# A graph attention kernel: which of the gathered tiles TensorE picks itself, one in 40 instead of one in 16

## What is computed

```python
for Wl, bl, Wr, br, att, bo, g, be in layers:            # three times
    xl = (h @ Wl + bl).reshape(n, H, C)                  # H * C = 128
    xr = (h @ Wr + br).reshape(n, H, C)
    x_i = xl[dst]                                        # neighbours in the sorted list
    x_j = xr[src]                                        # any row: a gather
    logit = einsum('ehc,hc->eh', leaky_relu(x_i + x_j, 0.2), att)
    alpha = softmax of logit over the edges of one dst
    out = segment_sum(alpha[..., None] * x_j, dst)
```

## Time and profile before

| | us |
|---|---|
| median of 3 runs (6605.31 to 6611.03) | 6605.85 |
| the profiled execution's own time | 6615.38 |
| its span, first to last instruction | 6613.6 |
| granted TensorE clock, mean over the span | 0.841 |
| PE busy | 4770.9 (72%) |
| DVE busy | 3963.6 (60%) |
| POOL busy | 3805.8 (58%) |
| ACT busy | 1607.7 (24%) |

### The profile page before, as it was taken

How to read it: one execution, slowest core, us unless ns; L and a number is a source line. 1 busy time by engine, 2 the same in 40 slices (tenths; PEclk the granted TensorE clock), 3 DMA queues, 4 the chain that set the end, 5 groups by cost and what they waited for, 6 DMA issues and landing times. The chain is left out here.

```text
span 6613.6 us, 138303 instructions
## 1 busy us (share of the span) xinstructions
PE 4770.9 (72%) x35731; PEld 4233.1 (64%) x35732; DVE 3963.6 (60%) x9254; ACT 1607.7 (24%) x3395; POOL 3805.8 (58%) x3122
## 2 busy tenths in 40 slices
PE   7878774888888748888887478888874566666665
PEld 5755334777787647778776478777773455555555
DVE  8987226666666576666665766666666533333334
ACT  4764100111111111111111111111111134444443
POOL 0000003777777737777777277777771078888884
PEclk9999986898999878999998789898886777777777
DMA  6853442333333323333333233333331222222221
GB/s 163 220 161 110 121 119 56 87 93 91 97 97 94 96 68 87 92 96 96 93 94 97 69 82 97 92 94 91 92 99 42 52 69 65 65 66 66 65 65 46
DMA packets 640422, 603.10 MB, mean 91 GB/s; under 512 B 245196, under 2 KB 579098, under 8 KB 639526
## 3 DMA queue, kind: packets, MB, share of 16 engines
q0 software_dynamic: 248480, 231.25, 15.1%
q10 hardware_dynamic: 234095, 211.99, 11.0%
q1 hardware_dynamic: 157719, 158.28, 9.0%
HBM read 498.50 MB, written 99.35 MB: 90 GB/s over the span
## 5 line engine op out<-in xcount | busy, mean ns | idle before, releaser
L563 POOL DMA_INDIRECT rows<-row_table,now x2250 | 2783.6, 1237 | 1780.7 <-issue 1505.8
L563 POOL DMA_INDIRECT rows<-node_table,now x800 | 989.0, 1236 | 563.5 <-issue 563.5
L850 PE MATMUL turn<-xr,ft 125*125 125x132 f32 x7500 | 969.7, 286 | 70.5 <-DVE ft L920 69.2
L850 PEld LDWEIGHTS turn<-xr,ft 125*125 125x125 f32 x7500 | 936.3, 197 | 76.2 <-DVE ft L920 71.1
L951 DVE SCALAR_TENSOR_TENSOR z<-zp,own 125x512 f32<-125x512 f32 x672 | 464.1, 691 | 780.8 <-PE zp L831 775.7
L842 PEld LDWEIGHTS sums<-both,hot 125*125 125x125 f32 x5376 | 765.5, 198 | 179.3 <-issue 117.4
L842 PE MATMUL sums<-both,hot 125*125 125x137 f32 x5376 | 795.5, 293 | 99.1 <-ACT both L737 57.7
L831 PE MATMUL zp<-rows,ident 125*125 x2700 | 809.9, 426 | 37.7 <-SPq L588 37.7
L828 PE MATMUL zp<-parts,hot_t 125*125 x8100 | 649.9, 232 | 240.2 <-issue 190.1
L828 PEld LDWEIGHTS zp<-parts,hot_t 125*125 125x125 bf16 x8100 | 607.9, 144 | 275.0 <-issue 273.2
L736 ACT CAST hot<-hot 125x500 f32<-125x500 bf16 x672 | 408.7, 608 | 1510.8 <-PE sums L842 898.8
(11 more groups left out here) (454 smaller groups left out, 5572.7 us busy)
## 6 DMA issues: line engine op xcount, KB each, us to landing
hot<-hots ACTq DMA_DIRECT2D x896, 122.1 KB
hot_t<-hots_t ACTq DMA_DIRECT2D x678, 122.1 KB
counts<-pairs SPq DMA_DIRECT2D x55, 685.1 KB
rows<-row_table,now POOLq DMA_INDIRECT x2250, 3.6
spread_slots<-slot_table POOLq DMA_DIRECT2D x56, 488.3 KB, 5.4
hots_t<-hot_t SPq DMA_DIRECT2D x112, 218.8 KB
hots<-hot_dst SPq DMA_DIRECT2D x112, 218.8 KB
pairs<-cells SPq DMA_DIRECT2D x25, 685.1 KB
```

Source lines behind the costliest of these rows:

```text
L563: pool.indirect_dma_start(rows[:, q, j, :], None, table, bass.IndirectOffsetOnAxis(ap=now[:, n, lane + j:lane + j + 1], axis=0)).then_inc( ...
L850: ins = pe.matmul(mixture, hot_n[:, w, :], xr[:, w, :], start=w == 0, stop=w == WIN - 1)
```

## The change

A tile is picked in every tenth quad instead of every fourth, so that TensorE makes 20 tiles per attention layer instead of 50, and POOL gathers 780 instead of 750. In blocks 0 to 8 the picks stand in the first two of the four groups of steps (`PER = 2`); blocks 9 to 13 have none. Two tiles are still made ahead of block 0 (`FIRST = 2`). The loops over a block's groups are split on all engines into groups with and without a pick. The list of picked sources, made once in the first stage, is cut from the other half of each row of 1000 edges, so that one small instruction there works on 250 numbers per partition instead of 125 (L1984), and the list's place in memory moved.

```diff
-PICK = 4
+PICK = 10
+PER = 2
+FIRST = 2
 PICKS = QUADS // PICK
-LAST = (PICKS - 2) // GROUP
+LAST = (PICKS - FIRST) // PER
...
-            def load_srcs(t, n=GROUP):
+            def load_srcs(t, n=PER):
...
+            def block_of(b, per):
+                if per:
+                    with act.Fori(0, per) as i:
+                        group(b, i)
+                        store_picked(PER * b + i + FIRST)
+                if per < GROUP:
+                    with act.Fori(per, GROUP) as i:
+                        group(b, i)
                 weigh(b)
...
-            def block_of(b, picking, picked_by):
-                four_steps(b, 0, softmax(b - 1, picked_by=picked_by), picking)
-                with pe.Fori(1, GROUP) as i:
-                    four_steps(b, i, None, picking)
+            def block_of(b, per, picked_by):
+                four_steps(b, 0, softmax(b - 1, picked_by=picked_by), per > 0)
+                if per > 1:
+                    with pe.Fori(1, per) as i:
+                        four_steps(b, i)
+                if per < GROUP:
+                    with pe.Fori(max(per, 1), GROUP) as i:
+                        four_steps(b, i, None, False)
                 sum_rows(BSTEPS * b - 1, AHEAD - 1)
 
             with pe.Fori(1, LAST) as b:
-                block_of(b, True, GROUP * b + 2)
+                block_of(b, PER, PER * b + FIRST)
             with pe.Fori(LAST, BLOCKS) as b:
-                block_of(b, False, PICKS)
+                block_of(b, 0, PICKS)
...
+            def block_of(b, per):
+                both(b, 0, per > 0)
+                if per > 1:
+                    with dve.Fori(1, per) as i:
+                        both(b, i, True)
+                if per < GROUP:
+                    with dve.Fori(max(per, 1), GROUP) as i:
+                        both(b, i, False)
...
-    g.picked_src = nc.dram_tensor("picked_src", (PICKS + GROUP, P), F16, kind="Internal").ap()
     g.picked_rows = nc.dram_tensor("picked_rows", (PICKS, P, ROW), F32, kind="Internal").ap()
     g.features = nc.dram_tensor("features", (D, N), F32, kind="Internal").ap()
+    g.picked_src = nc.dram_tensor("picked_src", (PICKS + PER, P), F16, kind="Internal").ap()
...
-                sp.dma_start(g.picked_src[0:PICKS, :], src16[1:RROWS:2, :]).then_inc(kept, 16)
+                sp.dma_start(g.picked_src[0:PICKS, :], src16[4:RROWS:5, 1, :]).then_inc(kept, 16)
...
-                link(dve.tensor_scalar(src16[:, :], src_row[:, rlen - P:rlen], float(-(N // 2)), None, ALU.add))
+                link(dve.tensor_scalar(src16[:, :, :], src_row[:, :].rearrange("r (h e) -> r h e", h=2)[:, :, rlen // 2 - P:rlen // 2], float(-(N // 2)), None, ALU.add))
```

More of the change, by code:

```diff
@@ L48 @@
 EPS = 1e-5
[L49 removed]
+PICK = 10
+PER = 2
+FIRST = 2
 PICKS = QUADS // PICK
 CUTS = ((0, 9), (9, 17), (17, WIN))
[L52 to L53 removed]
+LAST = (PICKS - FIRST) // PER
+assert RING % PICK == 0 and FIRST <= GROUP and PER <= GROUP and E // RROWS == 2 * HALF * P and FIRST + PER * LAST == PICKS and LAST < BLOCKS - 1
 GROUPS = (WIN + 3) // 4
@@ L761, in weigh @@
                 act.wait_ge(soft, SOFT * b + SOFT)
-            load_srcs(0, 2)
+            load_srcs(0, FIRST)
             for q in range(2):
                 load_spread(q, q)
-            lay(0, 2)
+            lay(0, FIRST)
             act.wait_ge(laid, 1)
-            load_srcs(2)
-            for t in range(2):
+            load_srcs(FIRST)
+            for t in range(FIRST):
                 store_picked(t)
@@ L772, in _, with spreads @@
             act.wait_ge(laid, 2)
-            load_srcs(GROUP + 2)
-            with act.Fori(0, GROUP) as i:
+            load_srcs(PER + FIRST)
+            def spreads(i):
                 for q in range(AHEAD):
                     load_spread(AHEAD * i + q + 2, (q + 2) % AHEAD)
-                store_picked(i + 2)
+            with act.Fori(0, PER) as i:
+                spreads(i)
+                store_picked(i + FIRST)
+            if PER < GROUP:
+                with act.Fori(PER, GROUP) as i:
+                    spreads(i)
             for q in range(2):
@@ L780, in _, with group @@
             weigh(0)
[L782 to L790, removed]
+            def group(b, i):
+                for q in range(AHEAD):
+                    k, c = BSTEPS * b + AHEAD * i + q, BSTEPS * b + AHEAD * i + q - BSTEPS
+                    widen(c, GROUP * b + i - GROUP, i, q)
+                    load_spread(k + 2, (q + 2) % AHEAD)
+                    load_hot(c + 2, (q + 2) % AHEAD)
+            def block_of(b, per):
[6 more added lines that the diff above has]
+                        group(b, i)
                 weigh(b)
@@ L878, in four_steps @@
                     k = BSTEPS * b + AHEAD * i + q
-                    if q or not isinstance(i, int):
+                    if q or not (isinstance(i, int) and i == 0):
                         sum_rows(k - BSTEPS - 1, (q - 1) % AHEAD)
@@ L883, in four_steps @@
                     if picking and q:
-                        pick(GROUP * b + i + 2, q - 1)
+                        pick(PER * b + i + FIRST, q - 1)
                     spread_rows(k + 1, GROUP * b + i + (q + 1) // AHEAD, (q + 1) % AHEAD, places[q])
-            for t in range(2):
+            for t in range(FIRST):
                 for r in range(len(CUTS)):
@@ L1029, in _, with alone @@
             dve.wait_ge(laid, 2)
-            with dve.Fori(0, GROUP) as i:
+            def alone(i, picking):
                 for q in range(AHEAD):
-                    choose(0, i, q)
+                    if picking:
+                        choose(0, i, q)
                     for _ in logits(AHEAD * i + q, i, q):
                         pass
+            with dve.Fori(0, PER) as i:
+                alone(i, True)
+            if PER < GROUP:
+                with dve.Fori(PER, GROUP) as i:
+                    alone(i, False)
             softmax(0)
             def both(b, i, picking):
-                first = isinstance(i, int)
+                first = isinstance(i, int) and i == 0
                 for q in range(AHEAD):
```

33 lines of the change are left out of this document (17 added, 16 removed).

## The result

The changed kernel takes 6551.32 us, the median of 4 runs (6548.67 to 6558.16). The kernel before took 6605.58 us on the same chip in the same session (4 runs, 6600.14 to 6611.03). The ratio is 0.9917, with a 95% interval of 0.9903 to 0.9930: 54 us, 0.8%, faster. The forecast was 79 us, with 36 to 97 us as its range. By its own range alone, without the part that was added for the first rival, it was 58 to 97 us.

What follows compares the result with a forecast made beforehand. POOL's gathers become the bound from block 1 on, in place of steps with picks and the softmax. Per layer 779 periods plus 3 us give 3615.0 against 3694.2 us together, 79 us less: 6527 us, range 6509 to 6570.

Steps and rivals of the forecast that it cites:

- first rival: Blocks 1 to 8: TensorE's lower clock or loop costs keep 87.9 us per block; 6596 us, half way 6566; chance 0.13.
- The bound changes hands: From block 1 on POOL becomes the bound and TensorE waits for it; blocks fall from 87.9 to 85.9 us.
- 46 us per layer for 30 gathers: Attention layers: 30 more gathers at 1.54 us each cost POOL 46 us per layer.
- the rule that I set against the change: 30 fetches per layer move from SyncE to GpSimd; the rule says SyncE or ScalarE issue is generally faster.
- The wait in block 0: At block 0's end POOL waits 3 us (0 to 7) for the first free slot in place of 15.7.
- my 8 us for two groups without picks: Block 0's last two groups lose their picks, saving 8 us, between 3.4 and 16.0 us.
- What lies outside the gathers: Before the first and after the last gather: stays, but for some 0.2 us more for the list of picked sources.
- From a profile to a median: The 79 us gain, found on a profiled execution 9.5 us above the median, was subtracted from the median 6605.9 us.
- POOL goes on waiting at each softmax: Ring full at each block's softmax: POOL waits 74 to 78 us per layer again, plus 46; 6744 us; chance 0.05.
- Dearer gathers: POOL's gathers without pauses cost say 1.60 us each, 46.7 us per layer; 60 us slower, 6666 us; chance 0.02.
- sign of being wrong: In the changed profile, a gather period above 1.55 us would show the forecast wrong; 1.54 us was forecast.

Runs made afterwards that it cites:

- thin kernels: The kernel before and the changed kernel, each with TensorE doing 3 of a picked tile's 25 matmuls: 6394.5 us (0.9678) and 6530.33 us (0.9876).
- pick20: The changed kernel with 10 picked tiles and 790 gathers per layer: 6583.29 us, ratio 0.9960 to the kernel before.
- second profile: The changed kernel run once more, unchanged: 6554.23 us, ratio 0.9911 to the kernel before.
- second pair: The kernel before and the changed kernel, both run once more unchanged: 6616.11 us and 6554.23 us.
- experiment 6: Both kernels once more, unchanged, for the scatter of a profile: before 6616.11 us (1.0017), changed 6554.23 us (0.9911).
- thin_before: The kernel before with TensorE doing 3 of a picked tile's 25 matmuls, 750 gathers per layer kept: 6394.5 us, ratio 0.9678.
- experiment 4: The changed kernel with its 20 picks placed four per block in blocks 0 to 3 and four tiles ahead of block 0: 6614.01 us, ratio 1.0004.
- experiment 7: Four more versions of the changed kernel on a third chip, where the kernel before takes 7057.29 us: 6709.86, 6895.99, 6917.48 and 6946.96 us.
- pick5_again: The kernel of pick5_three, unchanged, on the third chip: 6917.48 us, ratio 0.9799 to the kernel before.
- pick5_three: The changed kernel with 40 picks per layer, in three groups per block, four tiles ahead of block 0, 760 gathers: 6522.92 us, ratio 0.9871.

## Why the prediction came out as it did

**The bound changes hands: right.** POOL's waits at the softmaxes are gone, TensorE waits for landed rows in every block from 2 to 11 of layer 0, and blocks with and without picks take nearly the same time (85.9 and 84.3 us). The thin kernels and pick20 show it without help from the profile's releasers: most of TensorE's work on the picks is taken away and 21 us come back; gathers are added and their 1.54 us each come on top.

**46 us per layer for 30 gathers: right.** The thin pair gives 132.6 us for 90 gathers, forecast 3 x 46 = 138 us. The Trainium skill (page "DMA: Bandwidth & Descriptors", section "Issuing engine by pattern") says that transfers issued from SyncE or ScalarE are generally faster than those from GpSimd, but its table gives indirect transfers, and these gathers are indirect, to GpSimd. So the rule that I set against the change doesn't speak against it as plainly as I wrote. It doesn't decide here either: a block's time is the longer of two sums, and the picks were in the longer one.

**The wait in block 0: right in layer 0, too low in the others.** Forecast 3 us per layer (0 to 7), found 2.8, 6.8 and 6.6 us, and 4.3, 4.7 and 8.2 us in the second profile. The slot came free 1206.17 - 1082.6 = 123.6 us after the first gather in layer 0 and 126.5 us in the two others. Before it was 131.9, 131.3 and 130.8 us. So my 8 us for two groups without picks, which I took from layer 0's rows alone, came to 8.3 us there and to 4.7 and 4.4 us in the other two, where the first step also started 1.5 and 1.9 us later than before (block 0's steps fall from 59 us to 52.0, 54.2 and 53.9 us). The 8 us were a guess between 3.4 and 16.0 us, so the hit in layer 0 was partly luck. That is 7 us of the 25 that are missing.

**What lies outside the gathers: the term that I left out.** I set its change to nothing, since its code is all but the same, but in the profile of the change it is 9.9 us longer, and 1.6 us longer in the second pair. Some of this is scatter, but eight profiles are parted by 7.5 us in the mean without overlap (experiment 6). What in the change would cause it stays open.

**From a profile to a median: the largest single miss.** The profiled execution of before was 9.8 us above the median of its session, that of the change 1.7 us below. The account closes: 79.2 us forecast, less 3.6 us of gather time, less 9.9 us outside the gathers, less 11.5 us between profiles and medians, is 54.2 us, to the rounding the 54.3 us measured. Over both pairs the gather time fell by 75.6 and 61.8 us, 69 us in the mean; so about 10 us of the forecast were too much in the gathers, most of them block 0, the rest a period that was 0.003 us longer in the second profile than the one I used. Another 6 us, the mean of 9.9 and 1.6, are outside the gathers. The last 8 to 9 us lie between single profiled executions and the medians.

**The range held by luck in part.** The forecast's own range ended at 6548 us, and 6551.32 us lies just above it. It is inside 6509 to 6570 us because I had stretched that range toward the first rival, whose mechanism, long blocks of TensorE, didn't happen. The mechanism was right; the size, 79 us for 54, was too large by terms that the stretch was not made for.

**The rivals.** *TensorE keeps its block long:* the clock did fall, from 0.841 to 0.814 over the span, the way the Trainium skill has it (page "TensorE: Matmul & The Clock Gate", section "Part 1: The HAM clock gate": activity releases the higher level). I see no cost of it in blocks 2 to 11, which hold waits for rows, so that TensorE had the time; no run sets the clock apart from the rest. The rows, one for each kernel, before first:

```profile
core 0: 6613.6 us, clock 0.841
```

```profile
core 0: 6547.9 us, clock 0.814
```

*POOL goes on waiting at each softmax:* refuted by the waits of the change and by thin_before. *Dearer gathers:* refuted as a cost of 46 us, with 1.541 to 1.542 us in the three layers of the change, and 1.552 us at most in any layer of a repeat, which is scatter just above the 1.55 us that I had named as a sign of being wrong. What no rival of mine held is experiment 4: the same numbers of picks and gathers, with two more tiles ahead of block 0 and the rest in the first four blocks, would have gained nothing. My sum had that only inside the 8 us of block 0, and it was right by the placement that the change happens to have.

## What to carry to other kernels

When two engines work through the same blocks with a buffer between them, write down what a block costs each; taking work from the slower helps only until the other's sum is reached, here 2.5 of 10 us per block, and the best of the four splits tried on chips of the usual speed is the one where both are nearly equal (40 picks, 0.9871). Count the first block apart: once the supplier is the bound, whatever delays its first free slot lands on the span whole, and cost experiment 4 some 55 of the 60 us that it is slower than the change. And before a saving of one per cent is taken from one profiled execution, take a second one, since the profiled execution of the kernel before stood 9.8 us above its median, and two profiles of the change differed by 7 us outside the gathers and by 11 us in them.

## What I had not expected of the hardware

The same kernel took 6606 to 6616 us in the sessions of experiments 1 to 6 and 7057 us on the chip of experiment 7. POOL's gather took 1.54 us in all of them, and what lies outside the gathers took 2914.6 to 2931.5 us on the slow chip, as on the others: the loss is all between the first and the last gather of the attention layers (3984.2 us in pick5_again for 3589.3 in pick5_three). What shows there as slower is the hand-over from TensorE to VectorE. On the slow chip, in pick5_again, the spread ends at 1708.01 + 1.10 = 1709.11 and VectorE starts on it 1.72 us later, released by something that the profile calls remote, though this wait is for TensorE's count of spreads and for VectorE's own work, which was done:

```profile
1708.01 1.10 PE L846 MATMUL zp<-rows,ident 125*125 x4
...
1710.83 0.69 DVE L977 SCALAR_TENSOR_TENSOR z<-zp,own 125x512 f32<-125x512 f32 x1 [3.89 <-remote]
```

In pick5_three, the same program on the first chip, it starts 0.04 us after such an end:

```profile
1656.03 1.10 PE L846 MATMUL zp<-rows,ident 125*125 x4
...
1657.17 0.69 DVE L977 SCALAR_TENSOR_TENSOR z<-zp,own 125x512 f32<-125x512 f32 x1 [1.17 <-PE zp L846]
```

VectorE's waits from 1700 to 2000 us have 18 such cases in pick5_again and none in pick5_three:

```profile
DVE z L977 <- remote: 62.0, 18, 5.4
DVE z L977 <- PE zp L846: 30.5, 20, 3.8
```

Over the three layers 293 of the 478 such waits in pick5_again for which the trace holds the event end more than 0.5 us after the matmul's end, and 2 of 583 in pick5_three. In the late ones it is the semaphore's own event that comes late (2.4 us in the median), and VectorE starts 0.02 us after it, in the median of all these waits. Why it is late there stays open: no run of this study separates it from the work, one slow chip is all there is, and the profile models the ends of matmuls. And the ordinary gap between two gathers, 0.30 us, and their 1.21 us, both as medians, did not change with what the neighbours did: 3 matmuls per pick or 25, 10 picks or 50, waits or none.
